# Four of 17 key tiles' value product as three fp32r products of high and low parts

## What is computed

```python
def _L0_xattn_ref(x, latents, g1, b1, g2, b2, Wq, Wkv, Wout):
    ...
    xn = layer_norm(x, g1, b1)
    ln = layer_norm(latents, g2, b2)
    q = ln @ Wq
    kv_input = jnp.concatenate([xn, ln], axis=1)
    kv = kv_input @ Wkv
    k, v = jnp.split(kv, 2, axis=-1)
    ...
    logits = jnp.einsum('bhqd,bhkd->bhqk', q * scale, k * scale)
    w = jax.nn.softmax(logits.astype(jnp.float32), axis=-1).astype(logits.dtype)
    out = jnp.einsum('bhqk,bhkd->bhqd', w, v)
    out = out.transpose(0, 2, 1, 3).reshape(b, l, INNER)
    return out @ Wout
```

## Time and profile before

| what | value |
|---|---|
| median of 3 runs | 3170.88 us (3170.86 to 3171.22) |
| the profiled execution, its own time | 3172.66 us |
| its span | 3170.9 us |
| TensorE matmul busy | 2959.8 us, 93% |
| VectorE busy | 1973.7 us, 62% |
| ScalarE busy | 1349.4 us, 43% |
| GpSimd busy | 1062.9 us, 34% |
| value products, L1343 | 2176 records, 1113.7 us |
| row maxima, L1108 | 1024 operations, 683.2 us |

### The profile page before, as it was taken

How to read it: one execution, slowest core, us unless ns; L and a number is a source line. 1 busy time by engine, 2 the same in 40 slices (tenths; PEclk the granted TensorE clock), 3 DMA queues, 4 the chain that set the end, 5 groups by cost and what they waited for, 6 DMA issues and landing times. The chain is left out here.

```text
span 3170.9 us, 33934 instructions
## 1 busy us (share of the span) xinstructions
PE 2959.8 (93%) x11590; PEld 1852.5 (58%) x11590; DVE 1973.7 (62%) x3403; ACT 1349.4 (43%) x2312; POOL 1062.9 (34%) x838
## 2 busy tenths in 40 slices
PE   5757799999999999999999999999999999899997
PEld 2323456565666656566656565666666565676666
DVE  4698577876567777756687776565555554452225
ACT  4643254544354454535454544353443434211121
POOL 3078276654005666710176754000000000102113
PEclk8879699999999999999999999999999999899998
DMA  5343221212121121111221213011010100411112
GB/s 216 129 147 102 68 63 34 62 34 87 31 74 51 34 71 34 51 55 38 67 64 34 57 34 91 13 39 38 14 44 14 37 14 14 166 56 51 52 42 70
DMA packets 71679, 189.84 MB, mean 60 GB/s; under 512 B 8420, under 2 KB 39272, under 8 KB 63448
## 3 DMA queue, kind: packets, MB, share of 16 engines
q1 hardware_dynamic: 67096, 172.08, 18.1%
q0 software_dynamic: 3984, 15.60, 1.5%
q10 hardware_dynamic: 432, 0.01, 0.0%
HBM read 124.59 MB, written 28.44 MB: 48 GB/s over the span
## 5 line engine op out<-in xcount | busy, mean ns | idle before, releaser
L950 ACT ACTIVATE a_carry<-a_st 128x512 f32<-128x512 f32 (+1 forms) x1088 | 649.5, 597 | 1126.6 <-PE a_st L1331 1118.4
L1343 PE MATMUL a_o<-a_carry,a_vals 128*65 128x512 f32 (+1 forms) x2176 | 1113.7, 593 | 0.0
L1108 DVE TENSOR_REDUCE a_maxes<-a_mx 128x1 f32<-128x512 f32 x1024 | 683.2, 686 | 219.8 <-PE a_mx L1259 212.3
L1331 PE MATMUL a_st<-a_q,a_kone 65*128 65x512 f32 (+1 forms) x1088 | 431.8, 397 | 0.0
L847 POOL TENSOR_TENSOR a_shared<-a_shared,a_bc 128x512 f32<-128x512 f32 x192 | 251.6, 1310 | 384.7 <-DVE a_shared L1046 384.7
L1343 PEld LDWEIGHTS a_o<-a_carry,a_vals 128*65 128x65 f32 (+1 forms) x2176 | 284.2, 137 | 103.6 <-issue 1.8
L1330 PE MATMUL a_st<-a_q,a_keven 128*128 128x512 f32 (+1 forms) x544 | 326.0, 599 | 0.7 <-issue 0.7
L1330 PE MATMUL a_st<-a_q,a_kodd 128*128 128x512 f32 (+1 forms) x544 | 314.8, 579 | 0.0
L818 POOL TENSOR_TENSOR a_erstd<-a_emv,a_half 128x4 f32<-128x4 f32 x8 | 8.1, 1014 | 907.5 <-DVE a_emv L1134 907.5
L1259 PE MATMUL a_mx<-a_kodd,a_q 128*128 128x512 f32 x512 | 298.4, 599 | 7.3 <-DVE a_maxes L1108 6.4
L1046 DVE TENSOR_TENSOR_SCAN a_shared<-a_shared 128x512 f32<-128x512 f32 x192 | 289.1, 1508 | 12.7 <-POOL a_shared L836 11.6
(11 more groups left out here) (252 smaller groups left out, 4410.1 us busy)
## 6 DMA issues: line engine op xcount, KB each, us to landing
a_bc<-m_kept_bc SPq DMA_DIRECT2D x48, 512.0 KB, 3.7
a_wt<-a_w_split SPq DMA_DIRECT2D x15, 1536.0 KB, 9.9
a_kone<-a_keven SPq DMA_DIRECT2D x32, 528.5 KB, 4.5
a_kone<-a_kodd SPq DMA_DIRECT2D x32, 528.5 KB, 4.2
e_wall<-in_w_t_dram SPq DMA_DIRECT2D x27, 512.0 KB, 9.7
a_early<-m_kept_bc SPq DMA_DIRECT2D x16, 512.0 KB, 3.7
a_w_split<-a_wt POOLq DMA_DIRECT2D x4, 1536.0 KB, 5.5
a_shared<-in_ctx_dram SPq DMA_DIRECT2D x4, 1536.0 KB
```

What stands on the lines that cost most here:

```text
L950: nc.scalar.activation(p_of(s % 4)[0:r], st[0:r, s % 2], ACT.Exp, scale=SCALE).then_inc(exp_done, 1)
L1108: nc.vector.reduce_max(maxes[:, c, t:t + 1], mx[:, i % 2], AX_X).then_inc(mx_max, 1)
L1331: nc.tensor.matmul(st[0:r, s % 2], k_one[g % 2][0:DH + 1, kt * P:kt * P + r], qm[of(g)][0:DH + 1, :], start=False, stop=True).then_inc(st_ ...
L1343: nc.tensor.matmul(ps_o[0:DH + 1, g % 2], vals[0:r, kt * HG + j, :], p_of(s % 4)[0:r], start=(kt == 0), stop=(kt == KT - 1)).then_inc(pv_d ...
```

## The change

Of the 17 key tiles 1, 5, 9 and 13 (`SPLIT`) get another value product. Their V is kept as a high part in fp32r (`vals_high`, written by ScalarE from the projection's bank) and a low part (`vals_low`, VectorE: the projection minus the high part). Their exponentials are split in the same way: ScalarE copies them to fp32r (`p_high`) right behind the exponential, VectorE subtracts (`p_low`), as a new item `R` at the head of the list of the step after. TensorE then runs three fp32r products into the same accumulation: V high by p high, V low by p high, and, behind a wait for the low part, V high by p low. The product of the two low parts is left out. Since VectorE's V step now needs ScalarE's part, the V blocks with a split tile count among the high parts (`HIGH`), and each is evicted by a copy and a subtraction of one tile each.

```diff
+SPLIT = (1, 5, 9, 13)
...
-    at = {kt: [] for kt in range(KT)}
+    at = {kt: [("R", g, kt - 1)] if kt - 1 in SPLIT else [] for kt in range(KT)}
...
-HIGH = {x: i for i, x in enumerate(x for x in MADE if x[0] in "QK")}
+WHOLE = [i for i in range(KT) if i not in SPLIT]
+
+
+def has_split(what):
+    return what[0] == "V" and any(VB[what[2]][0] <= i < sum(VB[what[2]]) for i in SPLIT)
+
+
+HIGH = {x: i for i, x in enumerate(x for x in MADE if x[0] in "QK" or has_split(x))}
...
+                else:
+                    t, w = VB[i]
+                    if n > 0:
+                        act.wait_ge(pv_done, (n * HG - 1) * KT + t + w)
+                    for j in SPLIT:
+                        if t <= j < t + w:
+                            a = nc.scalar.activation(vals_high[:, SPLIT.index(j) * HG:(SPLIT.index(j) + 1) * HG, 0:DH],
+                                                     ring[:, k, (j - t) * GW:(j - t + 1) * GW].rearrange("p (a d) -> p a d", d=DH),
+                                                     ACT.Copy)
...
                 nc.scalar.activation(p_of(s % 4)[0:r], st[0:r, s % 2], ACT.Exp, scale=SCALE).then_inc(exp_done, 1)
+                if s % KT in SPLIT:
+                    act.wait_ge(exp_done, s + 1)
+                    nc.scalar.activation(p_high[:], p_of(s % 4), ACT.Copy).then_inc(p_high_ready, 1)
...
+                        if j in SPLIT:
+                            i = SPLIT.index(j) * HG
+                            o = nc.vector.tensor_tensor(vals_low[:, i:i + HG], own, vals_high[:, i:i + HG, 0:DH].bitcast(F32),
+                                                        ALU.subtract)
...
+            def low_exp(g, kt):
+                s = g * KT + kt
+                n = split_before(s)
+                dve.wait_ge(p_high_ready, n + 1)
+                nc.vector.tensor_tensor(p_low[:], p_of(s % 4), p_high[:].bitcast(F32), ALU.subtract).then_inc(p_low_ready, 1)
...
+                if kt in SPLIT:
+                    n, i = split_before(s), SPLIT.index(kt) * HG + j
+                    pe.wait_ge(p_high_ready, n + 1)
+                    nc.tensor.matmul(ps_o[0:DH + 1, g % 2], vals_high[:, i], p_high[:], start=False, stop=False)
+                    nc.tensor.matmul(ps_o[0:DH, g % 2], vals_low[:, i], p_high[:], start=False, stop=False)
+                    pe.wait_ge(p_low_ready, n + 1)
+                    nc.tensor.matmul(ps_o[0:DH + 1, g % 2], vals_high[:, i], p_low[:], start=False, stop=False).then_inc(pv_done, 1)
+                    return
```

More of the change, by code:

```diff
@@ L422, with split_before @@
 NX = TT * (len(KC) - 1) + 1
+SPLIT = (1, 5, 9, 13)
+def split_before(s):
+    g, kt = divmod(s, KT)
+    return g * len(SPLIT) + sum(i < kt for i in SPLIT)
 NU = CT * NS
@@ L580, in attention @@
         early = sb("a_early", [P, 6 * S + 2 * KVP + 32])
-        vals = sb("a_vals", [P, KT * HG, DH + 1])
+        vals = sb("a_vals", [P, len(WHOLE) * HG, DH + 1])
+        vals_high = sb("a_valshigh", [P, len(SPLIT) * HG, DH + 1], F32R)
+        vals_low = sb("a_valslow", [P, len(SPLIT) * HG, DH], F32R)
+        p_high, p_low = sb("a_phigh", [P, S], F32R), sb("a_plow", [P, S], F32R)
         o_sb = sb("a_osb", [P, 2, S])
@@ L620, in attention @@
         exp_done = sem("a_exp_done")
+        p_high_ready = sem("a_p_high_ready")
+        p_low_ready = sem("a_p_low_ready")
         pv_done = sem("a_pv_done")
@@ L807, in _ @@
             nc.gpsimd.memset(kvl[:, :, KV:KVP].bitcast(F32), 0.0)
+            nc.gpsimd.memset(vals_high[:, :, DH:DH + 1].bitcast(F32), 1.0)
             nc.gpsimd.memset(vals[:, :, DH:DH + 1], 1.0).then_inc(consts_set, 1)
@@ L1100, in low @@
                         dve.wait_ge(pv_done, (n * HG - 1) * KT + t + w)
-                    o = nc.vector.tensor_copy(vals[0:r, t * HG:(t + w) * HG, 0:DH], made)
-                o.then_inc(ring_free[k], 1)
+                    for j in range(t, t + w):
+                        own = made[:, (j - t) * HG:(j - t + 1) * HG]
+                        if j in SPLIT:
+                            i = SPLIT.index(j) * HG
+                            o = nc.vector.tensor_tensor(vals_low[:, i:i + HG], own, vals_high[:, i:i + HG, 0:DH].bitcast(F32),
+                                                        ALU.subtract)
+                        elif not has_split(what):
+                            at = WHOLE.index(t) * HG
+                            o = nc.vector.tensor_copy(vals[0:r, at:at + w * HG, 0:DH], made)
+                            break
+                        else:
+                            at = WHOLE.index(j) * HG
+                            o = nc.vector.tensor_copy(vals[0:r, at:at + HG, 0:DH], own)
+                o.then_inc(ring_free[k], 1)
+            def low_exp(g, kt):
[3 more added lines that the diff above has]
+                nc.vector.tensor_tensor(p_low[:], p_of(s % 4), p_high[:].bitcast(F32), ALU.subtract).then_inc(p_low_ready, 1)
             def row_max(g, i):
@@ L1146, in make @@
                     low(what)
+                elif kind == "R":
+                    low_exp(what[1], what[2])
                 elif kind == "X":
@@ L1341, in add_o @@
                     wait_evicted(pe, ("V", g // HG, i))
+                if kt in SPLIT:
[6 more added lines that the diff above has]
+                    return
                 pe.wait_ge(exp_done, s + 1)
-                nc.tensor.matmul(ps_o[0:DH + 1, g % 2], vals[0:r, kt * HG + j, :], p_of(s % 4)[0:r],
+                nc.tensor.matmul(ps_o[0:DH + 1, g % 2], vals[0:r, WHOLE.index(kt) * HG + j, :], p_of(s % 4)[0:r],
                                  start=(kt == 0), stop=(kt == KT - 1)).then_inc(pv_done, 1)
```

## The result

| | median, us | runs | lowest to highest |
|---|---|---|---|
| before | 3171.22 | 12 | 3170.31 to 3174.46 |
| changed | 3179.39 | 12 | 3169.83 to 3182.03 |

The ratio is 1.0017, with a 95% interval of 1.001 to 1.0025: the change makes the kernel slower, by 8.2 us if the medians are compared and by 5.5 us if the means are, just beyond no change and about at the 0.2% that the prediction took as the bound. The forecast was 3162. The profiled execution took 3179.55 us (span 3177.8), next to the median.

The account below looks back on a forecast made before the run. TensorE was taken to bound attention; -43.5 + 5.4 + 4 + 17.6 + 8 = -8.5 us gave 3164.2 against the profiled execution, 3162 against the median. The range was 3134 to 3184 us, the likeliest case's own 3150 to 3177.

Parts of the forecast that it names:

- What bounds the kernel: Attention, about 386 to 2700 us, lasts as long as TensorE's work, busy 2290 of 2314 us.
- TensorE, -43.5: 256 split-tile products in attention: three fp32r products at 0.23 us replace one of 0.86, gaining 0.17 each, -43.5 us.
- (a): Odd heads, K projection in steps 1 to 5: tile 1's saved 0.17 us goes into waiting for maxima, +5.4 us.
- (b): Every fourth head, step 10: V block 2 with tile 5, evicted ahead of two maxima, costs 0.25 us, +4 us.
- ScalarE and the waits at the split products: ScalarE's copies of exponentials and V, and waits for high and low parts in attention: costed at nothing.
- (c): 16 odd scan heads: low parts with port waits exceed VectorE's 1.3 us free, costing 1.1 us each, +17.6 us.
- (d): 16 even scan heads, VectorE 2.6 us free, GpSimd busy 16.5 of 18: low parts cost 0.5 us each, +8 us.
- The heads behind the scans (11 to 14 of a sample) free: Samples' heads 11 to 14, with their layer-norm work: counted as free, no cost.
- The clock: Sign of being wrong: a granted clock below 1.00 in the attention stage.
- rival C: Scan heads: shared port and VectorE become the bound, queues can grow; 3200 us, half-way 3181; chance 0.27.

## Why the prediction was wrong, point by point

- **What bounds the kernel:** right. The last sample, where VectorE has time, gained 9.7 us, and so do others as soon as low parts or GpSimd are gone.
- **TensorE, -43.5:** right. 0.23 per product; a last-sample even head gains 0.67 = 4 x 0.17.
- **(a) and (b), +5.4 and +4:** (a) right, (b) too high. The last sample's four means make 2.33 us per set of four heads, 37 for all sixteen sets instead of 43.5: its odd heads gain 0.15 to 0.18 less than the even ones, as (a) says, and (b) shows only as 0.02 (j=3 against j=1), so 6 was lost where 9.4 was put.
- **ScalarE and the waits at the split products, nothing:** right. No wait at them is in the trace, and the kernel without low parts, which keeps ScalarE's copies, gained 32 us.
- **(c) and (d), +17.6 and +8:** this is the step that failed. Against what the last sample's heads gain, the 33 scan heads lost 0.1 to 2.4 us each by the means of j: 3.6 for j=0, 21.5 for j=1, 13.9 for j=2 and 0.5 for j=3, **39 us instead of 25.6**. Three things were wrong in it. (i) The port wait was put at 0.28 per low part, the scan's mean excess; it measured 1.06 - 0.69 = 0.37, and the scans grew too, from 1.51 to 1.54. With three low parts a head that is 0.3 us more in each, up to 9 us in 32 heads. (ii) In (d) I took 0.5 near the low end, because maxima come singly; even heads with j=2 lost 1.5 each, those with j=0 0.4. The upper bound there, 1.4, was the right end for half of them. (iii) Rows 7 show head 17, but I read only its free time; the four layer-norm rows just before it, stretched beside GpSimd, were not in the sum, nor was the 0.74 us for which TensorE already stopped there behind the Q low parts. That place cost 9.2 of the 21.5 in heads 17 and 33, 3.4 of it by the clock.
- **The heads behind the scans (11 to 14 of a sample) free:** wrong by 5 us in this execution. Heads 29 and 45 lost 1.1 where 0.5 was to be gained; this 3.2 us is the stretch at the half clock behind a stop of 0.97 us, which other kernels pass at full clock, so it is chance. The other 1.7 is real: j=2 there gained 0.1 instead of 0.67, and TensorE stops for 1.15 us there behind VectorE's layer norm (L1059), where it stopped for 0.5 to 0.6 before.
- **The clock:** named only as a sign of being wrong. It was one: 7 us lie in the four stretches (all inside the sums above), half of them in heads 29 and 45.

In sum: -37 + 39 + 5 = +7, which is what the heads show (+6.8 together) and about what the medians do (+8.2). Against the forecast's -8.5, 39 + 5 stands for 25.6 and 6 for 9.4. The number is that of rival C half-way, 3181, in part by luck. Its argument, growing queues in even heads where GpSimd is at 16.5 of 18 us, fits the 17.5 us that even scan heads lost; but it loads all 32 heads alike, knows nothing of the layer-norm rows in heads 17 and 33, and its 3181 holds nothing for the 3.2 us of chance. C got too little weight because VectorE's reserve was costed per head, by its idle time, without asking how much of its busy time was already being held up by GpSimd. The pair with GpSimd cut shows that this counted.

Open stays why scan heads with j=3 lose nothing although they have the same K projection as those with j=1. Their low parts may fall beside other phases of the scans; no run moved the scans to try it. Why the move stops the kernel before for 1.6 us in heads 27, 43 and 59 is seen (1.9 us of statistics ahead of the last maxima), but a place without cost was not found.

## What to carry to other kernels

A VectorE operation with two SBUF inputs is priced by what GpSimd does at that moment, not by its duration elsewhere: here 0.69 us alone, 1.06 beside it, and it can lengthen GpSimd's operation as well (1.61 for 1.28). When work is moved from a full engine to one that is free on average, gather the gain per stage, and apply the change only in the stages where the receiving engine is free; here 28 heads without scans, 16 of them in the last sample, kept 13.6 us, where the split in all 64 heads lost time. A short wait in the profile before (0.74 us, once) marks the place where the same work, a little later, stops the engine for four times as long. Before choosing the low end of a cost, take GpSimd's work out of both kernels once: that pair of runs says what its presence is worth in all, and exchanging one input for PSUM says how much of that is the instruction's own.

## What the runs showed of the hardware

- Rows with one SBUF tensor and two per-partition scalars in SBUF (L1192, 128 x 256) took 1.3 us each beside GpSimd, 0.35 to 0.41 without it: they are held up too, not only operations on two tensors.
- TensorE's clock was granted at 1.2 GHz for 3.4 us behind a stop of 2.9 us in the middle of a dense stage, and also behind stops of 0.97 us (heads 29 and 45 of the changed kernel, but not 13) and 1.60 us in some heads but not in others: with the items moved, the kernel before stops for 1.60 us in three heads alike, and only behind the first of them is the clock lower (windows of that kernel, the first and the second such head):

```profile
1399.30:1402.70 3.40, 3.40 (x10) 2.06 (x11) 1.01 (x3) 0.10 (x1) 0.31 (x1) 0.55 0.00 0
1996.50:2003.00 6.50, 4.89 (x27) 3.36 (x26) 3.63 (x12) 1.19 (x2) 1.02 (x1) 1.00 0.01 3
```

So a stop can cost its own length and up to 1.7 us more, and a single profile doesn't tell whether the next execution pays it.
